# Which engine applies the layer norm: 256 normalised tiles moved from GpSimd's queue into VectorE's

## The reference, cut to what matters

```python
x = x + attention_a(layernorm(x))   # scores from distances of 3-d positions, causal
x = x + ffn(layernorm(x))           # sigmoid(xr Wr) * (relu(xk Wk)**2 Wv), x mixed with the token before
x = x + attention_b(layernorm(x))   # 16 heads of 16 channels, causal softmax
x = x + ffn(layernorm(x))

def _layernorm(x, axis=-1, eps=1e-05):
    m = jnp.mean(x, axis=axis, keepdims=True)
    v = jnp.var(x, axis=axis, keepdims=True)
    return (x - m) / jnp.sqrt(v + eps)
```

## Time and profile before

| what | us |
|---|---|
| median of 3 runs | 2155.03 (2154.79 to 2160.26) |
| the profiled execution's own time | 2155.86 |
| its span, first to last instruction | 2154.1 |
| busy: PE / PEld | 1852.8 (86%) / 921.0 (43%) |
| busy: DVE / ACT / POOL | 1427.4 (66%) / 1245.4 (58%) / 1027.3 (48%) |
| mean granted TensorE clock | 0.941 of full speed |

### The profile page before, as it was taken

How to read it: one execution, slowest core, us unless ns; L and a number is a source line. 1 busy time by engine, 2 the same in 40 slices (tenths; PEclk the granted TensorE clock), 3 DMA queues, 4 the chain that set the end, 5 groups by cost and what they waited for, 6 DMA issues and landing times. The chain is left out here.

```text
span 2154.1 us, 32514 instructions
## 1 busy us (share of the span) xinstructions
PE 1852.8 (86%) x9842; PEld 921.0 (43%) x9842; DVE 1427.4 (66%) x4173; ACT 1245.4 (58%) x2673; POOL 1027.3 (48%) x1074
## 2 busy tenths in 40 slices
PE   4476799889998899988998899978998899988986
PEld 3344344434543355434544345424554345323423
DVE  2235767766786677776776676776876677777732
ACT  0722655685648655595557755495557756465562
POOL 4364254436662465435753366534753357314314
PEclk8778699999999999999999999999999999999988
DMA  3006010211223111311123111311123102322000
GB/s 103 1 8 140 1 31 23 67 30 30 40 88 60 31 30 55 74 31 30 41 74 74 30 21 49 89 31 30 31 77 79 24 11 40 98 47 44 1 21 20
DMA packets 64348, 97.27 MB, mean 45 GB/s; under 512 B 15656, under 2 KB 58030, under 8 KB 58031
## 3 DMA queue, kind: packets, MB, share of 16 engines
q1 hardware_dynamic: 64174, 95.20, 20.1%
HBM read 61.09 MB, written 33.55 MB: 44 GB/s over the span
## 5 line engine op out<-in xcount | busy, mean ns | idle before, releaser
L852 ACT ACTIVATE pt<-exp_bank 128x512 f32<-128x512 f32 (+3 forms) x1536 | 748.2, 496 | 664.7 <-PE exp_bank L822 657.5
L867 DVE CUSTOM_DVE_ANT_0 max_bank<-max_bank,mask 128x128 f32<-128x128 f32 (+3 forms) x1024 | 501.4, 501 | 402.1 <-PE max_bank L811 387.7
L811 PE MATMUL max_bank<-ks,qs 96*128 96x512 bf16 (+3 forms) x1536 | 517.9, 342 | 81.4 <-DVE piece_max L870 45.0
L822 PE MATMUL exp_bank<-qs,ks 98*128 98x512 bf16 (+3 forms) x1536 | 512.6, 340 | 69.2 <-ACT pt L852 67.0
L870 DVE TENSOR_REDUCE piece_max<-max_bank 128x1 f32<-128x512 f32 x512 | 343.5, 685 | 105.6 <-PE max_bank L811 102.3
L837 PE MATMUL o_bank<-pt,v 128*17 128x512 f32 (+3 forms) x3072 | 335.6, 510 | 7.6 <-ACT pt L852 3.1
L353 POOL TENSOR_SCALAR xh<-xs,mv,rstd 128x256 f32<-128x256 f32 x256 | 321.2, 1261 | 10.0 <-PE side L379 3.8
L811 PEld LDWEIGHTS max_bank<-ks,qs 96*128 96x128 bf16 x1536 | 150.6, 98 | 382.7 <-DVE piece_max L870 136.5
L889 POOL TENSOR_SCALAR_AFFINE_SELECT pt<-pt 128x512 f32<-128x512 f32 x256 | 170.4, 666 | 291.6 <-ACT pt L852 291.3
L822 PEld LDWEIGHTS exp_bank<-qs,ks 98*128 98x128 bf16 x1536 | 151.9, 100 | 281.4 <-ACT pt L852 174.6
L505 POOL TENSOR_TENSOR sq<-sq 128x512 f32<-128x512 f32 (+1 forms) x96 | 95.9, 999 | 230.1 <-ACT sq L451 230.1
(11 more groups left out here) (94 smaller groups left out, 2284.0 us busy)
## 6 DMA issues: line engine op xcount, KB each, us to landing
parts_dram<-parts SPq DMA_DIRECT2D x64, 384.0 KB, 2.6
qs<-parts_dram SPq DMA_DIRECT2D x192, 128.0 KB, 7.1
ks<-parts_dram SPq DMA_DIRECT2D x32, 384.0 KB, 4.7
xs<-in_L_attn_a_x_dram SPq DMA_DIRECT2D x16, 512.0 KB, 4.2
ks<-parts_dram SPq DMA_DIRECT2D x32, 256.0 KB, 5.4
out_dram<-xs SPq DMA_DIRECT2D x16, 512.0 KB, 3.0
ks<-parts_dram SPq DMA_DIRECT2D x32, 128.0 KB, 5.9
qs<-neg_maxT SPq DMA_DIRECT2D x64, 8.0 KB, 1.9
```

Source lines behind the costliest of these rows:

```text
L811: pe.matmul(max_bank[u % MAX_BANKS][:, 0:k1 - k0], qs[r][0:KROWS, j, P * tile:P * (tile + 1)], ks[r][0:KROWS, j, k0:k1], start=True, stop= ...
L822: pe.matmul(exp_bank[k % EXP_BANKS][:, 0:q1 - q0], ks[r][:, j, P * kt:P * (kt + 1)], qs[r][:, j, q0:q1], start=True, stop=True).then_inc(s ...
L852: act.activation(pt[:, e % 2, j, 0:q1 - q0], exp_bank[k % EXP_BANKS][:, 0:q1 - q0], ACT.Exp, scale=SCALE).then_inc(exp_done, 1)
L867: dve.tensor_tensor_reduce(scores, scores, mask[:, HALF - w:HALF], 1.0, LOWEST, ALU.add, ALU.max, piece_max[:, j, m:m + 1]).then_inc(max_f ...
```

## The change

The four operations that write `xh` leave `pool_normalise` and stand at the end of `dve_statistics`, at the same quarters 7 to 10, with the same operands and the same two waits ahead of the first (for `rstd`, and for PE's transposes of the layer norm before). The power stays on POOL, in a function that is now called `pool_deviation`. No other function changes.

```diff
             last.then_inc(ln_step, 1)
             dve.wait_ge(ln_step, base + 2)
             dve.tensor_scalar(var_eps[:, r, :], mv[:, r, :, 1], EPS, None, ALU.add).then_inc(ln_step, 1)
-
-        def pool_normalise(at, s, n, h):
+            for t in range(TPH):
+                yield at(7 + t)
+                if t == 0:
+                    dve.wait_ge(rstd_ready, q + 1)
+                    if q > 0:
+                        dve.wait_ge(tr_full, 2 * q)
+                dve.tensor_scalar(xh[:, t, :], src[:, TPH * h + t, :], mv[:, r, t, 0:1], rstd[:, r, t:t + 1],
+                                  ALU.subtract, ALU.mult).then_inc(xh_ready, 1)
+
+        def pool_deviation(at, s, n, h):
             pool, q = nc.gpsimd, LN_AT[s, n, h]
             r, src = q % 2, xs[n % X_BUFFERS]
             yield at(6)
             pool.wait_ge(ln_step, 3 * q + 3)
             pool.tensor_tensor(rstd[:, r, :], var_eps[:, r, :], minus_half[:, :], ALU.pow).then_inc(rstd_ready, 1)
-            pool.wait_ge(rstd_ready, q + 1)
-            if q > 0:
-                pool.wait_ge(tr_full, 2 * q)
-            for t in range(TPH):
-                yield at(7 + t)
-                pool.tensor_scalar(xh[:, t, :], src[:, TPH * h + t, :], mv[:, r, t, 0:1], rstd[:, r, t:t + 1],
-                                   ALU.subtract, ALU.mult).then_inc(xh_ready, 1)
...
-                return [pool_normalise(at, s, n, h)] + ([pool_ffn(at, s, n, h)] if s in ("ffn2", "ffn4") else body)
+                return [pool_deviation(at, s, n, h)] + ([pool_ffn(at, s, n, h)] if s in ("ffn2", "ffn4") else body)
```

## The result

The changed kernel takes 2175.59 us (median of 4 runs, 2172.2 to 2179.85) against 2154.91 for the kernel before in the same comparison: ratio 1.0093, 95% interval 1.0064 to 1.0121. It is slower by about 20 us, outside the predicted range of 2137 to 2164. Its profiled execution took 2172.70 us, span 2171.0, at a mean granted clock of 0.943; the execution that the earlier trace rows come from had 2154.1 and 0.941. So the mean clock does not explain the difference.

The account below looks back on a forecast made before the run. TensorE (PE), busy 1852.8 of 2154.1 us, was taken as the bound, its idle time as what could change. 2155.86 - 20.7 gained at the ends + 13.4 added in the middle = 2148.6 (2147.8 on the median's scale); range 2142 to 2149, 8-in-10 2137 to 2164.

Parts of the forecast that it names:

- The start: Before full attention, PE's waits for `xh` on one serial chain shrink: 13.1 us gained, bounds 9 and 16.
- the end's figure: Tail's two last halves gain 6.4 us (3.3 and 3.1); one tail stretch in the middle adds 1.2.
- the price of a tile: Each `xh` tile on DVE costs x = 0.37 us, own cost plus wait for POOL, ends 0.21 and 0.58.
- between 0 and 0.23 I take 0.09: Wait for POOL added to each DVE tile: 0.09 us; the first of four tiles bears most.
- the tile's own 0.28 us: A tile's own cost on DVE in a row of tiles: 0.28 us, between 0.21 and 0.35.
- The other four stretches have gaps and cost nothing: Four of a batch's eight stretches have DVE gaps, so tiles cost nothing; without that cover, 4x each.
- x = 0.37: Price in us of one tile on DVE; with it six batches in the middle cost 13.4 us.
- rival 1: No change that can be told: the middle gives back what the ends win, x from 0.38 to 0.56; chance 0.34.
- 72x - 13.2: Cost in us of six batches in the middle, x the tile price; a batch costs 12x - 2.2.
- the working gives 10 x 0.35 - 0.8 = 2.7: Middle batch costs: FFN 4's second half 3x - 0.5, projection's first half 3x - 0.2, attention 1's first half 4x - 0.1.
- Rival 2: Port lock: every DVE tile waits 0.35 us for POOL, x 0.63, total 2166 us; chance 0.19 with rival 4.
- Rival 4: DVE stands at the power: 1 us in four full stretches of six batches, 24 us; chance 0.19 with rival 2.

Follow-up runs that it names:

- run 7: Kernel before, with `xh` tiles on DVE only for the first 8 and last 4 of 64 layer norms; unedited repeat for a second profile: 2135.83 us, ratio 0.9899.
- run 5: Kernel before plus four idle bn_stats on DVE in the quarters where the changed kernel applies tiles, POOL keeping the tiles: 2174.92 us, one run.
- run 1: Changed kernel with DVE's layer norm tiles ahead of the other stage work in each quarter: 2150.35 us, ratio 0.9978.
- run 3: Changed kernel with POOL's residual additions shortened to one channel of 256: 2152.21 us, one run.
- its control: Kernel before with the same residual additions shortened to one channel of 256: 2146.51 us, one run.
- run 9: Changed kernel with POOL's residual addition held until DVE's tile of the same quarter is done: 2164.53 us, one run.
- runs 2 and 7: One program, two executions: kernel before with tiles on DVE only for the first 8 and last 4 of 64 layer norms; 2141.79 and 2135.83 us.

## Why the prediction was wrong

1. **The start was right; the end's figure is in part luck.** Start 13.1 us predicted, 14.3 measured, in much the predicted shares: the first half came 3.1 us earlier (3.2 predicted), the projection's second half 10.9 (10.1), the next batch's first half 14.7 (13.1). The tail and the stretch before it gave 9.9 against 6.4 + 1.2, but that all of it is work is not shown. Of it 5.1 come between matmuls 1426 and 1535, where the kernel before had 10.2 us at the lower clock level and the changed one none; run 7, with the same tiles there and 10.2 us at that level, gained 2.1. Behind matmul 1535 it was 37.5 us before and 30.9 after. In the last half the wait for `xh` fell by 2.1 us only (3.1 predicted): two of its tiles met the addition there too, and took 1.36 and 1.35 us. What the work alone gave at the end stays open.
2. **The step that failed is the price of a tile, in the sentence "between 0 and 0.23 I take 0.09".** Its other term, the tile's own 0.28 us, was near: at 35.73 the first two tiles take 0.73 us together in DVE's timeline, 0.33 for the second. But the wait for POOL was taken as a mean, spread over all tiles and lowered because POOL would be less busy. It is not left to chance: it is set by the order of the program, and the emptier POOL's queue is, the sooner the addition starts beside the tile. On 6 of the 32 tiles of a batch it is 0.95 us (1.36 - 0.41), and on most others nothing. The mean of 584 ns lies just past the upper end of 0.58, but a mean does not price it, since the six lie in stretches where DVE leads PE.
3. **"The other four stretches have gaps and cost nothing"** failed for the tightest. FFN 4's first half had 1.16 us of gap; two meetings take 1.9 us, and it lost 1.14 in every batch.
4. **By stretch,** predicted with x = 0.37 and measured: FFN 4's first half 0 and 1.14; its second half 0.6 and 1.79; projection's first half 0.9 and 2.33; attention 1's first half 1.4 and 0.77; attention 1's second half -0.7 and -0.36. Six batches of the three kinds make 31.6 of the 41.1 us, attention 1's two halves some 2.5; the other 7 lie mostly after attention 1's second half, where the granted clock varies, and their cause stays open. (In rival 1's bounds, 72x - 13.2 at x = 0.56 is 27.1, not 27.2.)
5. **Rival 2 was the right mechanism with the wrong objection.** "POOL's longest work near these stretches was the `xh` tiles themselves" is true of the kernel before; but the addition stayed, and the change took away what had stood in POOL's queue ahead of it. The rival's price, 0.35 us on each of four tiles, should have been 0.95 on two. The Trainium skill (SBUF — State Buffer, Who interferes with whom) says that whoever issues first holds the shared ports for the whole instruction and the other is blocked fully. The trace agrees: a tile that started 0.50 us into a 1.71 us addition ended 0.15 us behind it.
6. Rival 4, DVE standing at the power, did not occur: none of DVE's waits for it lies in the full middle.

DVE's own time in the full stretches was even overpriced: run 5 shows that much the same DVE time without the meeting costs 1.4 us a batch in stretches for which the working gives 10 x 0.35 - 0.8 = 2.7. Whether the whole move would pay without the meetings is not shown: run 1, in which they are shorter, is 0.2% faster than the kernel before, but run 3 is 5.7 us slower than its control, with 17.1 to 23.9 us of a full batch at the lower clock level against the control's 10.2 to 13.7.

## What to carry to other kernels

When an operation moves to an engine that shares something with another, do not price the meeting by its mean: look in the program for what stands just ahead of it on the new engine, and which instruction of the other engine that releases. Taking work off an engine also starts its remaining work earlier, and possibly beside something new. Move only the instances that someone waits for (here 18 of the 64 layer norms, the ends and attention 1's second half), and leave the others where they are hidden.

## What the runs showed that was not expected

- **The meeting costs both sides.** POOL's addition has a median of 1706 ns in the changed kernel against a shortest of 1260: it starts at 1046.44 while DVE's mix runs until 1047.02, and takes 0.45 us more. With the addition held back (run 9) its mean is 1309. DVE's mixes beside POOL's tiles were slowed too, 0.93 us at 1045.10 before and 0.74 after.
- **One program's batch lengths differ by up to 4.4 us between executions,** with the granted clock (runs 2 and 7), mostly in the stretch after attention 1's second half. What decides it was not found; for differences of 5 us in a total, the comparison by matmul numbers was the safer instrument.
